# Image attention: the last 32 keys of four sub-steps gathered by GpSimd and turned by one transpose, and ScalarE evicts a transpose ahead of the next exponential

## The chip, the cores and the metric

The kernel runs on one core of a Trainium2 chip. The metric is the device time in microseconds (us) of one execution. TensorE (PE; its weight loads are shown apart as PEld), VectorE (DVE), ScalarE (ACT), GpSimd (POOL) and SyncE (SP) each run their own instructions in program order, and wait for each other by semaphores.

## The reference, cut to what matters

A chain of eight blocks (four cross-attentions, four feed-forward parts) updates x (4 batches of 512 tokens of 128 channels). The change touches the first block alone, an attention of 16 heads of 64 channels. Its queries come from x; its keys and values from the 154 context rows and the 512 rows of x together, so each query weighs 666 keys:

```python
kv_in = jnp.concatenate([x, l], axis=1)          # 154 context rows, 512 rows of x
k, v = jnp.split(kv_in @ Wkv, 2, axis=-1)        # 16 heads of 64
w = jnp.einsum('bhqd,bhkd->bhqk', q * scale, k * scale)
w = jax.nn.softmax(w, axis=-1)                   # over 666 keys
out = jnp.einsum('bhqk,bhkd->bhqd', w, v)
...
x = x + tanh(g_xattn[0]) * (out @ Wo)
```

## The kernel before, in words

This attention is called the image stage. Its work is cut into **sub-steps**, numbered i = 0 to 255: one sub-step is 128 queries of one head of one batch against all 666 keys. Four sub-steps (two heads h, two query tiles j) make a **unit** u, two units a **group** n (a pair of heads, `image_sub`). Keys are numbered 0 to 511 for x and 512 to 665 for the context, cut into KT0 = 6 tiles of 128; the sixth holds the last 26 keys. Values, scaled queries and probabilities are held in two bf16 parts, a high one and a low one (the remainder), and every product is the sum of three matmuls; "low" in a name is the remainder.

Every engine runs one loop over steps i (`image_steps`), and what it does in a step belongs to different sub-steps, so the pipeline is written out by hand. In step i:

- **PE** (`image_pe`): the scores of sub-step i into bank pair i % 2 (L683); in steps with i % 4 = 0 half of the weighing of unit i // 4 - 2 (tiles 0 to 2, L709, 18 matmuls), and in steps with i % 4 = 2 the other half (tiles 3 to 5, L709, 18 matmuls), then two transposes of the row of 1/sum (L615); then six transposes of the probabilities of sub-step i - 2 (`image_turn_pe`, L694: four into bank 4, two into bank 5); in even steps a quarter of the projections of the next group (L475, into bank 7, `side`).
- **DVE** (`image_ve`): in steps with i % 4 = 3 first the product with 1/sum (L740, `mixed`, which waits for ACT's `spread_kept`); then the row maximum of the scores of i (L744); in odd steps the remainders of the quarter that was projected (L798 to L813, `image_lows_ve`); in steps with i % 4 = 0 the reciprocal of the sums (L752, `inverted`); then the copy of bank 5 (L758, `kept_b`, 128x256), and for the first sub-step of a unit the remainder as well (L763, `low_c`).
- **ACT** (`image_ac`): the exponential of i (L837), which waits for DVE's maximum; in steps with i % 4 = 2 `spread_kept` (L846); the copy of bank 4 for sub-step i - 2 (L852, `kept_a`, 128x512); in even steps the quarter that was projected (L881 to L895).
- **POOL** (`image_po`): in steps with i % 4 = 0 first 1/sum spread over the heads' columns (L934, which waits for DVE's reciprocal) and the remainder of `mixed` (L942); then the remainders of the probabilities of sub-step i - 3 (L963: `low_a` 128x512, and `low_b` 128x256 in three of four sub-steps); then, in steps with i % 4 = 0 from 32 on, a piece of splitting the next block's weights (L979 to L983, 16 chunks in all).

For most steps nothing else is issued. A few hold **chores** (`image_chores`, `image_late`): the two normalizations of the next batch, its columns, the output projection of a batch that is done, and, near the end, the first routing steps of the next block. By their tables they touch 20 of the 64 units.

A step's name below is i % 4: **step 2** is the one with the second half of the weighing, and it turns a sub-step with i % 4 = 0. **Step 1** turns the fourth sub-step of a unit.

## Time and profile before

| | us |
|---|---|
| median of 3 runs | 1929.69 |
| lowest and highest | 1927.9 and 1934.78 |
| the profiled execution, its own time | 1934.83 |
| its span | 1933.0 |
| image stage, first to last exponential | 36.5 to 706.6 |
| PE busy in the span | 1515.4 (78%) |
| DVE, ACT, POOL busy in the span | 1205.2, 802.1, 757.9 |

In the views below an operation stands with its line, its engine, what it writes and reads, and its shape. A time in brackets behind it is the idle time of its engine just before it, with the work that ended that idle time. Starts are microseconds from the start of the span. A row of several instructions ("x6") spans from the first one's start to the last one's end, and the next row can start up to 0.1 us earlier than that, since an engine's operations overlap a little.

### The profile page before, as it was taken

To read this page: it belongs to the slowest core of one execution; us is meant where nothing else is said; L and a number is where in the kernel's file an instruction comes from. 1 tells how busy PE (TensorE), PEld (TensorE's weight loads), DVE (VectorE), ACT (ScalarE), POOL (GpSimd) and SP (SyncE) were. 2 spreads that over 40 slices of the span, in tenths; PEclk is the share of its full clock that TensorE was granted. 3 is DMA by queue.
4 is the path that set the end of the run, shared out by engine and by line. 5 is a ranking of instruction groups with operands and counts; after the bars stand their busy time and mean duration, and the time that the engine had idled before them with its cause. 6 is when DMAs were issued, how large, how long until landed. Compare 5 with 4: busy or idle time off the path is not lost.

```text
span 1933.0 us, 32091 instructions
## 1 busy us (share of the span) xinstructions
PE 1515.4 (78%) x11458; PEld 990.6 (51%) x11581; DVE 1205.2 (62%) x2958; ACT 802.1 (41%) x1806; POOL 757.9 (39%) x909
## 2 busy tenths in 40 slices
PE   4899989979998986574268789958976886478877
PEld 2677757766776665452155345523443333334544
DVE  5777667767766655547947657644465465676653
ACT  3677557747765644320035245533212452211111
POOL 3788668858755863510012342000002101143320
PEclk9999989999998997776558799989985697779887
DMA  6223211211211102400000000000000000000000
GB/s 243 76 87 106 76 52 42 55 35 41 53 38 42 51 20 84 150 20 1 0 1 1 11 4 2 1 1 1 1 1 1 1 1 1 1 1 6 1 6 12
DMA packets 35443, 63.94 MB, mean 33 GB/s; under 512 B 7527, under 2 KB 25026, under 8 KB 34131
## 3 DMA queue, kind: packets, MB, share of 16 engines
q1 hardware_dynamic: 33815, 59.77, 10.3%
q0 software_dynamic: 1472, 2.12, 0.3%
q8 instruction: 95, 1.56, 0.3%
q14 instruction: 61, 0.50, 0.1%
HBM read 30.59 MB, written 12.66 MB: 22 GB/s over the span
## 4 chain that ended last, share of the span: by engine, by line
PE 62%; DVE 24%; POOL 5%; issue 5%; ACT 3%; DMA 1%; SPq 0%; DVEq 0%; ACTq 0%; POOLq 0%
PE banks L475 14%; PE banks L694 8%; PE banks L709 6%; PE banks L683 6%; PE banks L1876 4%; DVE xn L421 3%; PE banks L1859 2%; PE banks L450 2%; POOL work L963 2%; PE banks L1785 1%; DVE norm_room L405 1%; PE banks L1826 1%; DVE work L744 1%; PE banks L2565 1%; PE banks L1516 1%
## 5 line engine op out<-in xcount | busy, mean ns | idle before, releaser
L963 POOL TENSOR_TENSOR work<-work 128x512 bf16<-128x512 f32 (+1 forms) x448 | 373.2, 863 | 47.6 <-ACT work L852 44.4
L837 ACT ACTIVATE work<-banks,work 128x666 f32<-128x666 f32 x256 | 209.2, 817 | 198.7 <-DVE work L744 163.3
L415 POOL TENSOR_TENSOR norm_room<-norm_room,minus_half 128x4 f32<-128x4 f32 x48 | 50.2, 1046 | 537.7 <-DVE norm_room L410 537.6
L744 DVE TENSOR_REDUCE work<-banks 128x1 f32<-128x666 f32 x256 | 216.1, 844 | 60.6 <-PE banks L683 60.1
L694 PE MATMUL banks<-const,work 128*128 128x128 f32 (+1 forms) x1536 | 218.5, 279 | 30.0 <-ACT work L852 25.8
L758 DVE COPY work<-banks 128x256 f32<-128x256 f32 x256 | 106.7, 417 | 123.7 <-PE banks L694 123.5
L694 PEld LDWEIGHTS banks<-const,work 128*128 128x128 f32 (+1 forms) x1536 | 156.5, 135 | 51.9 <-ACT work L837 29.3
L683 PE MATMUL banks<-work 128*128 128x154 bf16 (+1 forms) x932 | 172.2, 304 | 7.8 <-DMA work<-work 2.6
L475 PE MATMUL banks<-work,weights_b 128*128 128x512 bf16 (+1 forms) x830 | 157.2, 347 | 12.8 <-DVE work L2200 5.5
L709 PE MATMUL banks<-work 128*64 128x256 bf16 x2304 | 160.7, 284 | 7.5 <-POOL work L963 6.3
L852 ACT ACTIVATE work<-banks 128x512 f32<-128x512 f32 x256 | 151.3, 591 | 10.1 <-PE banks L694 9.8
L450 PE MATMUL banks<-const,xn 128*128 128x128 f32 x176 | 42.2, 385 | 135.8 <-DVE xn L421 83.8
L683 PEld LDWEIGHTS banks<-work 128*128 128x128 bf16 x1024 | 98.8, 99 | 86.0 <-issue 6.8
L456 ACT ACTIVATE xt<-banks 128x512 f32<-128x512 f32 x48 | 28.6, 597 | 267.8 <-PE banks L450 267.7
L1953 DVE TENSOR_REDUCE work<-banks 128x2 f32<-128x308 f32 x192 | 86.5, 472 | 83.2 <-PE banks L1831 45.3
L709 PEld LDWEIGHTS banks<-work 128*64 128x64 bf16 x2304 | 121.6, 111 | 28.3 <-POOL work L963 9.5
L475 PEld LDWEIGHTS banks<-work,weights_b 128*128 128x128 bf16 (+1 forms) x840 | 82.8, 100 | 83.1 <-issue 18.3
L2772 POOL TENSOR_TENSOR work<-work 128x512 bf16<-128x512 f32 x64 | 67.7, 1061 | 139.1 <-DVE work L2721 139.0
L1932 ACT ACTIVATE work<-banks 128x256 f32<-128x256 f32 (+1 forms) x256 | 87.4, 382 | 61.4 <-PE banks L1863 26.9
L450 PEld LDWEIGHTS banks<-const,xn 128*128 128x128 f32 x176 | 27.7, 193 | 148.5 <-DVE xn L421 77.6
L1859 PE MATMUL banks<-work 128*128 128x256 bf16 (+1 forms) x256 | 66.9, 293 | 14.4 <-ACT work L1924 11.6
L475 PE MATMUL banks<-weights_c 128*128 128x128 bf16 (+2 forms) x288 | 66.3, 261 | 0.0
(398 smaller groups left out, 3059.7 us busy)
## 6 DMA issues: line engine op xcount, KB each, us to landing
work<-work SPq DMA_DIRECT2D x128, 166.5 KB, 3.0
sorted<-in_pads SPq DMA_DIRECT2D x10, 838.5 KB
weights_b<-in_weights SPq DMA_DIRECT2D x1, 4120.0 KB, 23.4
work<-scratch SPq DMA_DIRECT2D x64, 64.0 KB, 2.0
weights_b<-in_weights SPq DMA_DIRECT2D x1, 2824.0 KB, 9.6
weights_a<-in_weights SPq DMA_DIRECT2D x1, 2056.0 KB, 8.1
weights_a<-in_weights SPq DMA_DIRECT2D x1, 2050.0 KB, 9.4
work<-work SPq DMA_DIRECT2D x32, 64.0 KB, 1.9
```

The costliest lines, as they stand in the source:

```text
L450: i = pe.transpose(ps[:, j * P:j * P + rows], src[0:rows, j, :], self.eye[0:rows, 0:rows])
L475: m = pe.matmul(out, left(a), right(b), start=start and n == 0, stop=stop and n == 2)
L683: m = pe.matmul(slot[:, a:z], lhs, k[:, h, part, a:z], start=part == 0, stop=part == 1)
L694: m = pe.transpose(ps[0:rows, c:c + P], prob[:, t * P:t * P + rows], self.eye)
L709: m = pe.matmul(self.out_bank[64 * h:64 * h + 64, 0:2 * P], self.v[n % 3][:, t, of_values, 64 * h:64 * h + 64], self.probs_parts[u % 2][:, ...
L744: ve.tensor_reduce(self.neg_max[i % 4], self.slot[i % 2][:, 0:KEYS0], AX_X, ALU.max, negate=True).then_inc(self.mark("max"))
L758: ve.tensor_copy(self.probs_t[u % 2][:, h, 4:KT0, j * P:(j + 1) * P], self.bank_b[:, 0:2 * P].rearrange("p (t n) -> p t n", t=2)).then_inc ...
L837: ac.activation(self.probs[i % 3], self.slot[i % 2][:, 0:KEYS0], ACT.Exp, bias=self.neg_max[i % 4], accum_out=self.sums[u % 4][:, 2 * j + ...
L852: ac.activation(self.probs_t[u % 2][:, h, 0:4, j * P:(j + 1) * P], self.bank_a.rearrange("p (t n) -> p t n", t=4), ACT.Copy).then_inc(self ...
L963: po.tensor_tensor(parts[:, :, :, 0], exact, parts[:, :, :, 1], ALU.subtract).then_inc(self.mark(event, i - 3))
L1859: m = pe.matmul(bank, left, a.q4[b % 2][:, g, cols], start=True, stop=s != 4)
L1932: ac.activation(out, self.bank_of(k, HALF)[0:rows_n, :], ACT.Exp).then_inc(self.mark("exp4", s, n))
```

## The change

Four things change, all of them in the image stage.

1. **The keys are cut in another way.** Tile 4 holds keys 512 to 633 (its other rows of values are zero), and the last 32 keys (634 to 665) are taken out. After the exponential of each sub-step, POOL copies its last 32 columns into 32 of the 128 columns of `rest` (L988 of the new kernel, `gathered`). When the fourth is there, one transpose turns all 128 (L700), in step 1, beside the fourth sub-step's own. A sub-step has five transposes of its own and no longer six.
2. **The weighing of these keys** is six matmuls of 128x128 over 128 columns for the unit (L722), in place of six of 64 columns of weights over 256 columns. The values lie in two extra tiles, zero outside of four blocks of 32x64 (`value_pieces`), so ACT and DVE each write five pieces in place of two in the third quarter of the projections. For each batch POOL lays the last 32 context columns out four times (`four_times`, two copies).
3. **Bank 5** holds one turned tile (128x128), copied by DVE for each sub-step, and in step 1 the gathered one, which DVE copies and takes the remainder of. POOL's `low_b` is 128x128, now for all four sub-steps. The exponential of i waits for `gathered` of i - 3, since the buffers of the probabilities take turns.
4. **ACT** issues `kept_a` of sub-step i - 2 ahead of the exponential of i, no longer behind it and behind `spread_kept`.

The diff, cut to its core:

```diff
@@ image_turn_pe
-        for bank, tiles, name in ((4, range(0, 4), "kept_a"), (5, range(4, KT0), "kept_b")):
-            ps = self.bank(pe, bank, *((name, i) if bank == 4 or (i % 4) else ("low_c", i // 4)))
...
+        ps = self.bank(pe, 4, "kept_a", i)
+        for t in range(4):
+            m = pe.transpose(ps[:, t * P:(t + 1) * P], prob[:, t * P:(t + 1) * P], self.eye)
+        m.then_inc(self.mark("turned_a"))
+        ps = self.bank(pe, 5, *(("kept_b", i) if i % 4 < 3 else ("low_c", i // 4)))
+        m = pe.transpose(ps[:, 0:P], prob[:, 4 * P:5 * P], self.eye)
+        if i % 4 == 3:
+            pe.wait_ge(*self.at("gathered", i))
+            m = pe.transpose(ps[:, P:2 * P], self.rest[i // 4 % 2], self.eye)
+        m.then_inc(self.mark("turned_b"))
@@ image_weigh_pe
-        if tiles[-1] == KT0 - 1:
+        if tiles[-1] == KT0 - 2:
+            rest = self.halves(self.rest_t[u % 2])
+            for of_values, of_probs in orders:
+                for j in (0, 1):
+                    m = pe.matmul(self.out_bank[:, j * P:(j + 1) * P], self.v[n % 3][:, KT0 - 1 + j, of_values, :], rest[:, :, of_probs],
...
@@ image_ve
-                ve.tensor_copy(self.probs_t[u % 2][:, h, 4:KT0, j * P:(j + 1) * P],
...
+                ve.tensor_copy(self.probs_t[u % 2][:, h, 4, j * P:(j + 1) * P], self.bank_b[:, 0:P]).then_inc(self.mark("kept_b", i - 2))
+                if (h, j) == (1, 1):
+                    whole = self.rest_t[u % 2]
+                    ve.wait_ge(*self.own("ve", ve.tensor_copy(whole, self.bank_b[:, P:2 * P])))
+                    ve.tensor_tensor(self.halves(whole)[:, :, 0], self.bank_b[:, P:2 * P], self.halves(whole)[:, :, 1],
                                      ALU.subtract).then_inc(self.mark("low_c", u))
@@ image_ac
         for i in self.image_steps():
+            if 2 <= i < SUBS + 2:
+                u, _, _, _, h, j = self.image_sub(i - 2)
...
+                ac.activation(self.probs_t[u % 2][:, h, 0:4, j * P:(j + 1) * P],
+                              self.bank_a.rearrange("p (t n) -> p t n", t=4), ACT.Copy).then_inc(self.mark("kept_a", i - 2))
             if i < SUBS:
                 u, _, _, _, h, j = self.image_sub(i)
                 if i >= 3:
                     ac.wait_ge(*self.at("turned_b", i - 2))
+                    ac.wait_ge(*self.at("gathered", i - 3))
@@ image_po
-                for tiles, event in (((0, 4), "low_a"), ((4, KT0), "low_b")):
+                for tiles, event in (((0, 4), "low_a"), ((4, KT0 - 1), "low_b")):
                     if event == "low_b":
-                        if (h, j) == (0, 0):
-                            continue
...
+            if 1 <= i < SUBS + 1:
+                u, s = (i - 1) // 4, (i - 1) % 4
+                if s == 0 and u >= 2:
+                    po.wait_ge(*self.at("turned_b", 4 * u - 4))
+                po.wait_ge(*self.at("exp", i))
+                po.tensor_copy(self.rest[u % 2][:, 32 * s:32 * (s + 1)], self.probs[(i - 1) % 3][:, KEYS0 - 32:]).then_inc(self.mark("gathered", i - 1))
@@ image_lows_ve (image_keep_ac likewise)
+            for tile, rows, cols, src in self.value_pieces():
+                ve.tensor_tensor(v[rows, tile, 1, cols], side[rows, src], v[rows, tile, 0, cols], ALU.subtract).then_inc(self.mark("v_low"))
+    def value_pieces(self):
+        out = [(KT0 - 2, slice(0, CTX - 32), slice(0, P), slice(2 * P, 3 * P))]
+        for h, j in ((0, 0), (0, 1), (1, 0), (1, 1)):
+            r, c = 32 * (2 * h + j), 64 * h
+            out.append((KT0 - 1 + j, slice(r, r + 32), slice(c, c + 64), slice(3 * P + c, 3 * P + c + 64)))
+        return out
```

ACT, end of step 1 to step 2 of one unit, before (L837 exponential, L852 `kept_a`, L846 `spread_kept`, L895 a projected quarter):

```order
199 L852 ACTIVATE work<-banks 128x4x128 [waits turned_a,weighed]
200 L837 ACTIVATE work<-banks,work 128x666 [waits max,turned_b]
201 L846 ACTIVATE work<-banks 128x256 [waits spread_turned]
202 L852 ACTIVATE work<-banks 128x4x128 [waits turned_a,weighed]
203 L895 ACTIVATE work<-banks 128x4x128 [waits projected]
```

The same place of the changed kernel (L861 exponential, L851 `kept_a`, L870 `spread_kept`, L912 the quarter):

```order
200 L861 ACTIVATE work<-banks,work 128x666 [waits max,low_b,turned_b]
201 L851 ACTIVATE work<-banks 128x4x128 [waits turned_a,weighed]
202 L861 ACTIVATE work<-banks,work 128x666 [waits max,low_b,turned_b]
203 L870 ACTIVATE work<-banks 128x256 [waits spread_turned]
204 L912 ACTIVATE work<-banks 128x4x128 [waits projected]
```

In step 2 `kept_a` stood third, behind the exponential and `spread_kept`; it stands first now, and both stand behind it.

POOL, step 0 of one unit and its weight piece, before (L934 spread of 1/sum, L942 remainder of `mixed`, L963 remainders of probabilities):

```order
108 L934 COPY work<-work 128x256 [waits inverted,spread_turned]
109 L942 TENSOR_TENSOR work<-work 128x256 [waits mixed]
110 L963 TENSOR_TENSOR work<-work 128x4x128 [waits kept_a]
111 L963 TENSOR_TENSOR work<-work 128x2x128 [waits kept_b]
112 L979 CAST split<-weights_b 128x512 [waits split]
```

The same place of the changed kernel (L953, L961, L982 are those three lines, L988 the gathering copy):

```order
159 L953 COPY work<-work 128x256 [waits inverted,spread_turned]
160 L961 TENSOR_TENSOR work<-work 128x256 [waits mixed]
161 L982 TENSOR_TENSOR work<-work 128x4x128 [waits kept_a]
162 L982 TENSOR_TENSOR work<-work 128x128 [waits kept_b]
163 L988 COPY work<-work 128x32 [waits exp]
164 L1013 CAST split<-weights_b 128x512 [waits split]
```

The copy that gathers a unit's fourth sub-step stands behind the four others of step 0.

PE, from the transposes of step 1 to the second half of the weighing in step 2, before:

```order
573 L694 MATMUL banks<-const,work 128x128 [waits kept_a,exp]
574 L694 MATMUL banks<-const,work 128x128 x3
575 L694 MATMUL banks<-const,work 128x128 [waits kept_b]
576 L694 MATMUL banks<-const,work 26x128
577 L683 MATMUL banks<-work 128x512 [waits exp,dma_head01]
578 L683 MATMUL banks<-work 128x512
579 L683 MATMUL banks<-work 128x154 x2
580 L709 MATMUL banks<-work 64x256 [waits low_c,low_b]
581 L709 MATMUL banks<-work 64x256 x17
582 L615 MATMUL banks<-const,work 128x128 [waits spread]
```

The same place of the changed kernel (`gathered` counts on the semaphore `low_b`):

```order
555 L694 MATMUL banks<-const,work 128x128 [waits kept_a,exp]
556 L694 MATMUL banks<-const,work 128x128 x3
557 L697 MATMUL banks<-const,work 128x128 [waits kept_b]
558 L700 MATMUL banks<-const,work 128x128 [waits low_b]
559 L686 MATMUL banks<-work 128x512 [waits exp,dma_head01]
560 L686 MATMUL banks<-work 128x512
561 L686 MATMUL banks<-work 128x154 x2
562 L716 MATMUL banks<-work 64x256 [waits low_c,low_b]
563 L716 MATMUL banks<-work 64x256 x11
564 L722 MATMUL banks<-work 128x128 x6
565 L616 MATMUL banks<-const,work 128x128 [waits spread]
```

The sixth transpose of step 1 waits for POOL's copy, and the scores of the next step stand behind it.

## Rows read from the trace of the kernel before

**Rows 1.** Windows: stretch, length, busy of PE, PEld, DVE, ACT, POOL; PEclk; DMA.
```profile
30.00:716.00 686.00, 621.61 (x6091) 471.98 (x6189) 472.83 (x1033) 447.12 (x1029) 500.89 (x649) 0.97 0.20 56
...
215.00:220.00 5.00, 4.19 (x44) 3.35 (x45) 2.33 (x5) 2.19 (x5) 1.94 (x3) 1.00 0.01 2
```

**Rows 2.** One line of code: L846 on ACT, one instruction a unit.
```profile
L846 ACT ACTIVATE work<-banks x64: 372/375/385, 66.2 to 715.7; 128x256 f32<-128x256 f32 x64
```

**Rows 3.** Timeline of ACT (start, length, line, shape, idle before): two L846.
```profile
75.97 0.38 ACT L846 ACTIVATE work<-banks 128x256 f32<-128x256 f32 x1
...
204.35 0.38 ACT L846 ACTIVATE work<-banks 128x256 f32<-128x256 f32 x1
```

**Rows 4.** Timeline of PE's weight loads, one unit from 302.60.
```profile
302.60 0.61 PEld L694 LDWEIGHTS banks<-const,work 128*128 128x128 f32 x6
...
307.23 0.59 PEld L694 LDWEIGHTS banks<-const,work 128*128 128x128 f32 x6 [0.35 <-issue]
...
309.09 0.60 PEld L694 LDWEIGHTS banks<-const,work 128*128 128x128 f32 x6
309.70 0.64 PEld L683 LDWEIGHTS banks<-work 128*128 128x128 bf16 x4
310.47 0.94 PEld L709 LDWEIGHTS banks<-work 128*64 128x64 bf16 x18
...
311.81 0.61 PEld L694 LDWEIGHTS banks<-const,work 128*128 128x128 f32 x6
```

**Rows 5.** Timeline of ACT in step 2 of that unit.
```profile
302.79 0.82 ACT L837 ACTIVATE work<-banks,work 128x666 f32<-128x666 f32 x1 [0.30 <-DVE work L744]
...
303.59 0.38 ACT L846 ACTIVATE work<-banks 128x256 f32<-128x256 f32 x1
303.86 0.60 ACT L852 ACTIVATE work<-banks 128x512 f32<-128x512 f32 x1
304.34 0.61 ACT L895 ACTIVATE work<-banks 128x512 bf16<-128x512 f32 x1
305.72 0.82 ACT L837 ACTIVATE work<-banks,work 128x666 f32<-128x666 f32 x1 [0.78 <-DVE work L744]
```

**Rows 6.** Timeline of DVE from step 2 to step 0 of that unit.
```profile
303.60 0.42 DVE L758 COPY work<-banks 128x256 f32<-128x256 f32 x1 [0.90 <-PE banks L694]
...
304.40 0.41 DVE L740 TENSOR_TENSOR work<-banks,work 128x256 f32<-128x256 f32 x1
304.78 0.85 DVE L744 TENSOR_REDUCE work<-banks 128x1 f32<-128x666 f32 x1
305.54 0.68 DVE L798 TENSOR_TENSOR work<-banks,work 128x512 bf16<-128x512 f32 x1
306.14 0.41 DVE L758 COPY work<-banks 128x256 f32<-128x256 f32 x1
306.47 0.84 DVE L744 TENSOR_REDUCE work<-banks 128x1 f32<-128x666 f32 x1
307.23 0.17 DVE L752 RECIPROCAL work<-work 128x4 f32<-128x4 f32 x1
```

**Rows 7.** Timeline of POOL in step 0 of that unit.
```profile
307.53 0.40 POOL L934 COPY work<-work 128x256 f32<-128x256 f32 x1 [1.44 <-DVE work L752]
307.89 0.62 POOL L942 TENSOR_TENSOR work<-work 128x256 bf16<-128x256 f32 x1
308.46 1.62 POOL L963 TENSOR_TENSOR work<-work 128x512 bf16<-128x512 f32 x2
310.01 0.61 POOL L979 CAST split<-weights_b 128x512 bf16<-128x512 f32 x1
```

**Rows 8.** Groups by shape, to 850 us: count, busy us, mean ns, idle before.
```profile
L963 POOL TENSOR_TENSOR work<-work 128x512 bf16<-128x512 f32 x256 | 267.8, 1046 | 47.6 <-ACT work L852 44.4
L963 POOL TENSOR_TENSOR work<-work 128x256 bf16<-128x256 f32 x192 | 119.0, 620 | 0.0
...
L921 POOL COPY context<-work 128x616 f32<-128x616 f32 x2 | 1.3, 701 | 0.0
```

More of the change, by code:

```diff
@@ L522, in image_memory @@
         self.k = [self.place(2, 2, KEYS0, dt=BF16) for _ in range(2)]
-        self.v = [self.place(KT0, 2, P, dt=BF16) for _ in range(3)]
+        self.v = [self.place(KT0 + 1, 2, P, dt=BF16) for _ in range(3)]
         self.probs = [self.place(KEYS0) for _ in range(3)]
@@ L526, in image_memory @@
         self.q_part = self.scratch[:, 2:4, :].rearrange("p t n -> p (t n)").bitcast(BF16)
-        self.probs_t = [self.place(2, KT0, 2 * P) for _ in range(2)]
+        self.probs_t = [self.place(2, KT0 - 1, 2 * P) for _ in range(2)]
+        self.rest, self.rest_t = ([self.place(P) for _ in range(2)] for _ in range(2))
         self.sums = [self.place(4) for _ in range(4)]
+        self.ctx_last = self.place(2, P, dt=BF16)
         self.inverse = [self.place(4) for _ in range(2)]
@@ L595, in image_pe @@
         pe.wait_ge(*self.at("dma_const", 16))
-        pe.wait_ge(*self.at("clean", 1))
         self.turn(pe, ("in", 0), self.xn[:, 0:QT, :], 0, ("in", 0, 1))
@@ L654, in image_project_pe @@
         elif part == 2:
-            self.bank(pe, 7, "v_low", 3 * n + 2)
+            self.bank(pe, 7, "v_low", 6 * n + 5)
             if n == 0:
@@ L662, in image_project_pe @@
             self.products(pe, side[:, 2 * P:3 * P], lambda s: c[:, s, c0:c0 + P], lambda s: values[s], True, True)
-            m = self.products(pe, side[:, 3 * P:4 * P], lambda s: c[:, s, c0 + P:c0 + 2 * P], lambda s: values[s], True, True)
+            if n % PAIRS == 0:
+                pe.wait_ge(*self.at("four_times", b))
+            m = self.products(pe, side[:, 3 * P:4 * P], lambda s: self.ctx_last[:, s, :], lambda s: values[s], True, True)
         else:
-            self.bank(pe, 7, "v_low", 3 * n + 3)
+            self.bank(pe, 7, "v_low", 6 * n + 6)
             for t in range(QT):
@@ L688, in image_turn_pe @@
         pe.wait_ge(*self.at("exp", i + 1))
-        for bank, tiles, name in ((4, range(0, 4), "kept_a"), (5, range(4, KT0), "kept_b")):
-            ps = self.bank(pe, bank, *((name, i) if bank == 4 or (i % 4) else ("low_c", i // 4)))
-            for t in tiles:
-                rows = min(P, KEYS0 - t * P)
-                c = (t - tiles[0]) * P
-                m = pe.transpose(ps[0:rows, c:c + P], prob[:, t * P:t * P + rows], self.eye)
-            m.then_inc(self.mark("turned_a" if bank == 4 else "turned_b"))
+        ps = self.bank(pe, 4, "kept_a", i)
[8 more added lines that the diff above has]
+        m.then_inc(self.mark("turned_b"))
     def image_weigh_pe(self, pe, u, tiles):
@@ L891, in image_keep_ac @@
                 v = self.v[n % 3]
-                ac.activation(v[:, 4, 0, :], side[:, 2 * P:3 * P], ACT.Copy).then_inc(self.mark("v_kept"))
-                ac.activation(v[0:CTX_REST, 5, 0, :], side[0:CTX_REST, 3 * P:4 * P], ACT.Copy).then_inc(self.mark("v_kept"))
+                for tile, rows, cols, src in self.value_pieces():
+                    ac.activation(v[rows, tile, 0, cols], side[rows, src], ACT.Copy).then_inc(self.mark("v_kept"))
         else:
@@ L967, in image_po, with four_times_po @@
             pass
+    def four_times_po(self, po, b):
+        if b:
+            po.wait_ge(*self.at("projected", 4 * (PAIRS * b - 1) + 3))
+        for s in (0, 1):
+            i = po.tensor_copy(self.ctx_last[:, s, :].rearrange("p (r k) -> p r k", r=4),
+                               self.ctxn_parts[:, s, (b + 1) * CTX - 32:(b + 1) * CTX].unsqueeze(1).to_broadcast([P, 4, 32]))
+        i.then_inc(self.mark("four_times", b))
     def image_x_low_po(self, po, b):
```

48 lines of the change are left out of this document (20 added, 28 removed).

## The prediction

> **What bounds the kernel now.** I read the windows first. Over the image stage PE is busy 621.61 of 686.00 us and POOL 500.89, DVE 472.83, ACT 447.12, at a granted clock of 0.97 [rows 1]. So PE is the busiest, but a change that lengthens a chain of waits between the engines can still take its place. The pace comes from `spread_kept`, which ACT issues once a unit: 64 of them from 66.2 to 715.7 us, so 10.31 us from one to the next on average [rows 2]. Where no chores fall, 14 units take 128.38 us, 9.17 us each [rows 3]. By the chores' tables 20 of the 64 units hold chores; 44 are clean.
>
> In a clean unit PE's weight loads follow each other nearly without a gap: from one step 2's first transpose to the next it is 302.60 to 311.81, 9.21 us, and the only gaps that a row names are 0.35 us ahead of the transposes of step 0 and one of 0.2 us inside the 1.34 us from the second half of the weighing to the transposes of step 2 (1.34 less 0.94 of loads and 0.20 for two transposes) [rows 4]. PE sets the pace there, and everything else has slack.
>
> **The change part by part.**
>
> *Transposes.* Six take 0.60 us, 309.09 to 309.70, or 0.10 each [rows 4]. Three of four sub-steps lose one; the fourth keeps six. That is 0.30 us a unit off the bounding engine.
>
> *Weighing.* 18 matmuls over 256 columns take 0.94 us of loads, 0.052 us each, and two of them run side by side in halves of the array [rows 4]. Six of the old form go, and six full-width ones over 128 columns come: the same number of columns through the array when pairs overlap. I take nothing, with 0.1 us a unit either way. The row shows a switch from half-width to full-width at about 0.2 us, and the change moves it from behind 18 matmuls to behind 12. The Trainium skill, TensorEngine Tiling (Array Packing), section Key Properties, says that a change of tiling mode drains the engine; by it alone a second drain would come if the six counted as another mode than the transposes behind them, and the sum would be 0.2 us a unit higher. The rows show none between bf16 and f32 work of full width: the loads of L683 begin 0.01 us after those of L694 end [rows 4].
>
> *ACT's order, seen from PE.* The gap of 0.35 us in step 0 [rows 4] is partly the wait for bank 4, which `kept_a` frees late because it stands behind an exponential that waits for DVE. With `kept_a` first it shrinks to the drain, 0.2: 0.14 us a unit. So **the gain is 0.44 us a unit**, if nothing else becomes late.
>
> *What becomes late: ACT.* In step 2 the first operation is now `kept_a`, which needs four transposes of that step. PE does them behind the weighing. In the trace DVE's copy of bank 5 starts 1.00 us after the first of six [rows 4, 6], so `kept_a` can start 0.80 after it (two transposes fewer), at 303.40 on the clock of before. The exponential had started at 302.79 [rows 5]; it now starts at 303.40 + 0.48 = 303.88, over a microsecond later. Behind it stands `spread_kept`, for it DVE's product (L740) waits at the head of step 3, and behind that both maxima, the reciprocal, and POOL's whole step 0. This is the wait that the change adds, and its queue.
>
> *What becomes late: POOL.* The sixth transpose of step 1 waits for a copy that POOL makes last in step 0. POOL begins that step only after DVE's reciprocal, even before the change [rows 7].
>
> *The loop.* These join into one chain which closes on itself in one unit. Each term is a distance between starts unless stated:
> - PE's first transpose in step 2 to `kept_a`: 0.80 (above); to the exponential: 0.48 (303.86 to 304.34 [rows 5]); to `spread_kept`: 0.80 (302.79 to 303.59 [rows 5]); its length 0.38 and the handover 0.09 (DVE's maximum ends at 305.63, ACT starts at 305.72 [rows 5, 6]): 2.55.
> - DVE [rows 6]: product 0.38, maximum 0.76, remainder of the quarter 0.60, copy of bank 5 0.33 less 0.13, maximum 0.76: 2.70. The 0.13 is my estimate for half the columns, the slope between 0.41 us for 256 columns and 0.85 for 666 being 1.07 ns a column. Reciprocal to POOL 0.30 [rows 6, 7]: 3.00.
> - POOL [rows 7, 8]: spread 0.36, remainder of `mixed` 0.57, the pair of remainders 1.55. The pair's second is 128x128 now: 1046 ns for 512 columns and 620 for 256 give 1.66 ns a column, so 0.21 less, 1.34. The gathering copy: 398 ns for 256 columns (the 0.40 of the row) and 701 for 616 give 0.21 us for 32. Sum 2.48.
> - Handover to PE 0.10, then the sixth transpose 0.10, scores 0.77, weighing, drain and 1/sum 1.34 [rows 4]: 2.31, and PE is at the first transpose of step 2 again.
>
> 2.55 + 3.00 + 2.48 + 2.31 = **10.34 us a unit**, against 9.17 now and 8.73 that PE would need. PE stands about 1.6 us in each unit at the sixth transpose; the 0.44 us that it saved is in that wait. +1.17 us x 44 clean units = 51 us. In the other 20, DVE's chores already keep PE waiting, and a part of the chain is hidden under them; bounds are 0 and 1.17 each, and I take the middle, 12 us. The five small pieces (three more instructions on ACT and on DVE in one quarter a group) lie where both have slack in this loop. Start and end of the stage: under 2 us. Sum +63: the profiled execution would go from 1934.83 to 1998, and the median, 5.1 lower, from 1929.69 to **1993**.
>
> Bounds. The copy can be 0.15 to 0.40 (its slope without a floor is under 0.05, and the whole 256-column one is 0.40), `low_b` between 0.41 and its old 0.62, DVE's copy between 0.20 and 0.33, the six matmuls 0.1 either way: T from 10.2 to 10.9. With 0 to the full rise in the 20 units: 1929.69 + 44 x 1.0 = 1974 up to 1929.69 + 64 x 1.7 = 2038; both ends at once are unlikely, and I keep 1974 to 2022 for this case.
>
> **The rivals.**
>
> *The gathering copy alone is late.* If the later exponential does not reach DVE's product in time to matter, the loop starts at the scores of step 3: maximum to POOL is 0.76 + 0.60 + 0.20 + 0.76 + 0.30 = 2.62, POOL and handover 2.58, PE to step 2's transposes 2.21, from them to the maximum's start 302.60 to 304.78 less one transpose, 2.08: 9.49 us [rows 4, 6, 7]. +0.32 x 44 and some in the rest: **1947**. Against it: nothing in the code lets L740 pass ahead of `spread_kept`, nor that ahead of the exponential. It holds if ACT's `kept_a` starts far sooner than 0.80 us after the first transpose.
>
> *PE stays the bound: faster.* 8.73 us a unit, -0.44 x 44 and half of it in the others: 19 + 4, **1906**. This needs the copy ready when PE has done five transposes of step 1, at 309.60 on the old clock. On that clock POOL starts step 0 at 307.53 and needs 2.48, so 310.0 at best; it decides from 0.4 us less on POOL. For it speaks only that POOL idles 1.44 us ahead of the step [rows 7], but it idles waiting for DVE.
>
> *No change.* The waits take just what the transposes give, as when POOL's step 0 is 0.3 us shorter than I have and the product is not late: **1930**.
>
> *The clock falls.* A PE that stands 15% of the time might be granted less. A window with 4.19 of 5.00 us busy still has 1.00 [rows 1], and the loop has 8.73 of 10.34, the same share. If it fell to half, PE would be the bound again far above 2022.
>
> **How the numbers follow.** The main case gets 0.66, the copy alone 0.13, PE the bound 0.11, no change 0.07, the clock or something worse than my bounds 0.03. The range that leaves out no more than 0.2 runs from 1942 to 2022: the main case and the copy alone. About 0.5% (10 us) is what a measurement of this kernel can tell from no change. Faster by more: 0.11; within: 0.07; slower: 0.82.
>
> **What the profile after would show.** `spread_kept` once every 10.3 us in clean stretches; PE's weight loads idle 1.3 to 1.8 us in front of the sixth transpose of step 1, released by POOL's copy; DVE idle ahead of the product for ACT's `spread_kept`, and no longer ahead of the maximum of step 3; ACT idle ahead of `kept_a` for PE's transposes; POOL's 128x32 copy at 0.2 us. If PE's wait is about 0.5 us and DVE starts step 3's maximum as the scores end, the second case holds. If no wait is there, POOL's step 0 began sooner than the reciprocal of before allowed, and I am wrong on DVE's order. The likeliest error of size is what the 20 units with chores do.

## The result, and the profile after

| | before | after |
|---|---|---|
| median, us | 1928.80 (1927.62 to 1934.78, 4 runs) | 1986.99 (1984.81 to 1991.53, 4 runs) |
| profiled execution, us | 1934.83 | 1984.81 |
| its span, us | 1933.0 | 1983.0 |

The ratio of after to before is 1.0303, with a 95% interval of 1.0288 to 1.0319. The change makes the kernel 3% slower. The forecast was 1993 us, in a range of 1942 to 2022.

From the page of the kernel after, parts 1, 4 and 5 (line, engine, operation, out<-in, count | busy us, mean ns of one | idle before and its releaser):

```profile
PE 1508.4 (76%) x11389; PEld 971.1 (49%) x11389; DVE 1194.2 (60%) x3117; ACT 816.3 (41%) x1902; POOL 780.4 (39%) x1237
...
PE 46%; DVE 26%; POOL 10%; issue 9%; ACT 6%; DMA 1%; ACTq 0%; SPq 0%; DVEq 0%; POOLq 0%
...
L851 ACT ACTIVATE work<-banks 128x512 f32<-128x512 f32 x256 | 154.3, 603 | 215.4 <-PE banks L694 214.4
```

PE still has most work, yet its share of the chain that ended last is 46% now, against 62% on the page of before. ACT idles 214 us in all in front of `kept_a` (L851), waiting for PE's transposes. The same two views as in [rows 1] and [rows 2], of after (windows: stretch, length, busy of PE, PEld, DVE, ACT, POOL, then PEclk; and one line of code):

```profile
30.00:716.00 686.00, 570.47 (x5573) 422.85 (x5574) 435.23 (x1127) 429.31 (x1050) 487.17 (x905) 0.97 0.20 55
...
L870 ACT ACTIVATE work<-banks x64: 374/384/386, 69.3 to 766.7; 128x256 f32<-128x256 f32 x64
```

All five engines are less busy in the same 686 us, PE by 51, and the granted clock is the 0.97 of before. Over the whole span PE and DVE have 7 and 11 us less work than before, ACT and POOL 14 and 22 us more, on engines that are busy less than half of the time. That doesn't make 50 us: the engines wait for each other. `spread_kept` starts its 64 units at 69.3 and ends them at 766.7, 697.4 us against 649.5 before [rows 2]. The difference is 48 us; 3 more are lost ahead of the first one. That is the 50 us by which the profiled executions differ.

Now one clean unit, link by link. PE's weight loads (start, length, line, shape, idle before with its releaser), from one step 2 to the next:

```profile
324.81 0.47 PEld L694 LDWEIGHTS banks<-const,work 128*128 128x128 f32 x4
...
329.05 0.42 PEld L694 LDWEIGHTS banks<-const,work 128*128 128x128 f32 x4 [0.20 <-issue]
...
331.20 0.14 PEld L697 LDWEIGHTS banks<-const,work 128*128 128x128 f32 x1
332.80 0.14 PEld L700 LDWEIGHTS banks<-const,work 128*128 128x128 f32 x1 [1.46 <-POOL work L988]
332.88 0.63 PEld L686 LDWEIGHTS banks<-work 128*128 128x128 bf16 x4
333.63 0.59 PEld L716 LDWEIGHTS banks<-work 128*64 128x64 bf16 x12
334.43 0.34 PEld L722 LDWEIGHTS banks<-work 128*128 128x128 bf16 x6 [0.21 <-issue]
334.73 0.20 PEld L616 LDWEIGHTS banks<-const,work 128*128 128x128 f32 x2
334.90 0.47 PEld L694 LDWEIGHTS banks<-const,work 128*128 128x128 f32 x4
```

ACT, DVE and POOL in the same unit:

```profile
325.61 0.60 ACT L851 ACTIVATE work<-banks 128x512 f32<-128x512 f32 x1 [1.79 <-PE banks L694]
326.11 0.81 ACT L861 ACTIVATE work<-banks,work 128x666 f32<-128x666 f32 x1
...
326.90 0.38 ACT L870 ACTIVATE work<-banks 128x256 f32<-128x256 f32 x1
```

```profile
327.31 0.42 DVE L750 TENSOR_TENSOR work<-banks,work 128x256 f32<-128x256 f32 x1 [1.29 <-ACT work L870]
327.65 0.84 DVE L754 TENSOR_REDUCE work<-banks 128x1 f32<-128x666 f32 x1
328.41 0.68 DVE L815 TENSOR_TENSOR work<-banks,work 128x512 bf16<-128x512 f32 x1
329.01 0.28 DVE L768 COPY work<-banks 128x128 f32<-128x128 f32 x1
329.21 0.84 DVE L754 TENSOR_REDUCE work<-banks 128x1 f32<-128x666 f32 x1
329.97 0.17 DVE L762 RECIPROCAL work<-work 128x4 f32<-128x4 f32 x1
```

```profile
330.26 0.40 POOL L953 COPY work<-work 128x256 f32<-128x256 f32 x1 [2.10 <-DVE work L762]
330.63 0.62 POOL L961 TENSOR_TENSOR work<-work 128x256 bf16<-128x256 f32 x1
331.20 1.40 POOL L982 TENSOR_TENSOR work<-work 128x512 bf16<-128x512 f32 x2
332.54 0.21 POOL L988 COPY work<-work 128x32 f32<-128x32 f32 x1
```

Read them as one ring: PE turns (324.81), ACT copies bank 4 (325.61), takes the exponential (326.11), writes `spread_kept` (326.90); DVE multiplies (327.31), finds a maximum, works off a quarter, copies bank 5, finds a second maximum, inverts (329.97); POOL does its step 0 (330.26) and the gathering copy last (332.54); PE, which has stood 1.46 us, makes the sixth transpose (332.80), the scores, the weighing, and turns again (334.90). Each idle time in the ring is released by the link ahead of it. It takes 10.09 us, and in the long stretches without chores nearly every unit has 10.09 or 10.10. An early unit, the one that ends with the `spread_kept` of 112.95 us, has one more operation on POOL ahead of the copy (L956, 1.04 us), and takes 11.09: 1.00 more, as a link of the ring would.

### The profile page after: what moved, and what is told of

The parts are those of the page before. It is cut to its first block, busy times and chain, and to the rows that moved or that the text cites. A ratio compares the mean times of both kernels' runs of the same rounds, so it can differ in the third digit from the quotient of the medians.

```text
span 1983.0 us, 32535 instructions
## 1 busy us (share of the span) xinstructions
PE 1508.4 (76%) x11389; PEld 971.1 (49%) x11389; DVE 1194.2 (60%) x3117; ACT 816.3 (41%) x1902; POOL 780.4 (39%) x1237
## 3 DMA queue, kind: packets, MB, share of 16 engines
q1 hardware_dynamic: 33815, 59.77, 10.1%
## 4 chain that ended last, share of the span: by engine, by line
PE 46%; DVE 26%; POOL 10%; issue 9%; ACT 6%; DMA 1%; ACTq 0%; SPq 0%; DVEq 0%; POOLq 0%
PE banks L475 11%; PE banks L1910 3%; POOL work L982 3%; PE banks L716 3%; ACT work L861 3%; DVE xn L421 3%; DVE work L754 2%; PE banks L686 2%; PE banks L1893 2%; PE banks L450 2%; POOL work L961 2%; PE banks L1819 1%; PE banks L694 1%; DVE norm_room L405 1%; PE banks L1860 1%
## 5 line engine op out<-in xcount | busy, mean ns | idle before, releaser
L982 POOL TENSOR_TENSOR work<-work 128x512 bf16<-128x512 f32 (+1 forms) x512 | 360.2, 728 | 32.3 <-ACT work L851 29.8
L851 ACT ACTIVATE work<-banks 128x512 f32<-128x512 f32 x256 | 154.3, 603 | 215.4 <-PE banks L694 214.4
L861 ACT ACTIVATE work<-banks,work 128x666 f32<-128x666 f32 x256 | 208.6, 815 | 37.5 <-DVE work L754 37.1
L686 PE MATMUL banks<-work 128*128 128x512 bf16 (+1 forms) x1024 | 191.1, 310 | 4.3 <-DMA work<-work 3.6
L694 PE MATMUL banks<-const,work 128*128 128x128 f32 x1024 | 160.7, 280 | 2.7 <-ACT work L851 2.7
L716 PE MATMUL banks<-work 128*64 128x256 bf16 x1920 | 138.8, 286 | 6.1 <-POOL work L982 4.2
L686 PEld LDWEIGHTS banks<-work 128*128 128x128 bf16 x1024 | 99.2, 100 | 85.9 <-issue 6.5
L768 DVE COPY work<-banks 128x128 f32<-128x128 f32 x256 | 72.1, 282 | 99.1 <-PE banks L697 61.6
L694 PEld LDWEIGHTS banks<-const,work 128*128 128x128 f32 x1024 | 114.1, 143 | 17.2 <-issue 15.9
L2806 POOL TENSOR_TENSOR work<-work 128x512 bf16<-128x512 f32 x64 | 67.7, 1061 | 138.8 <-DVE work L2755 138.6
L716 PEld LDWEIGHTS banks<-work 128*64 128x64 bf16 x1920 | 100.2, 110 | 25.1 <-POOL work L982 7.2
L700 PE MATMUL banks<-const,work 128*128 128x128 f32 x64 | 21.2, 332 | 89.0 <-POOL work L988 89.0
L953 POOL COPY work<-work 128x256 f32<-128x256 f32 x64 | 25.7, 402 | 136.8 <-DVE work L762 136.8
```

The source lines that it names most:

```text
L686: m = pe.matmul(slot[:, a:z], lhs, k[:, h, part, a:z], start=part == 0, stop=part == 1)
L694: m = pe.transpose(ps[:, t * P:(t + 1) * P], prob[:, t * P:(t + 1) * P], self.eye)
L716: pe.matmul(self.out_bank[64 * h:64 * h + 64, 0:2 * P], self.v[n % 3][:, t, of_values, 64 * h:64 * h + 64], self.probs_parts[u % 2][:, h, ...
L768: ve.tensor_copy(self.probs_t[u % 2][:, h, 4, j * P:(j + 1) * P], self.bank_b[:, 0:P]).then_inc(self.mark("kept_b", i - 2))
L851: ac.activation(self.probs_t[u % 2][:, h, 0:4, j * P:(j + 1) * P], self.bank_a.rearrange("p (t n) -> p t n", t=4), ACT.Copy).then_inc(self ...
L861: ac.activation(self.probs[i % 3], self.slot[i % 2][:, 0:KEYS0], ACT.Exp, bias=self.neg_max[i % 4], accum_out=self.sums[u % 4][:, 2 * j + ...
```

## The experiments

Each kernel differs from the one named by the edit shown. Medians differ by up to 9 us from chip to chip (1928.58 to 1937.41 for before), so times are compared through the ratio to runs of before on the same chip. The length of a unit is read from ACT's timeline, from one `spread_kept` to the next.

### The two halves of the change apart

**e1: after, with ACT's order as before.**

```
 for i in self.image_steps():
-    kept_a of step i-2
     exponential of step i
     spread_kept
+    kept_a of step i-2
```

> The changed kernel with kept_a back behind the exponential and spread_kept, all else kept. Theory (one loop through ACT's order and through POOL's gathering copy, 10.10 us a clean unit): without ACT's part the loop starts at the scores of step 3, 2.61 on DVE + 2.28 on POOL + 0.26 handover + 2.10 to the transposes of step 2 + 2.01 to the next maximum = 9.26 us a clean unit, total 1935 to 1945 us, PE still stands 0.4 to 0.6 us at the sixth transpose. Rival A (the copy alone makes the loss): stays near 1987. Rival B (ACT's order alone makes it): back to 1929 or, with the transposes saved, 1910.

Measured: ratio 1.0136 (1.0099 to 1.0173), or 1955 us on the 1928.80 of before, above the range that I had expected. Units of 9.25 and 9.97 us alternate. The short one has the length expected, but e4 below has it too, without the copy at the end of POOL's step: the agreement with 9.26 does not show that the copy sets it. The long one I had not foreseen. It comes in units with the five pieces of values. PE's loads, ACT and DVE in a long unit of e1, on the way to its long wait:

```profile
216.60 0.42 PEld L694 LDWEIGHTS banks<-const,work 128*128 128x128 f32 x4 [0.95 <-ACT work L854]
```

```profile
211.94 1.16 DVE L830 TENSOR_TENSOR work<-banks,work 122x128 bf16<-122x128 f32 x5
213.13 0.29 DVE L768 COPY work<-banks 128x128 f32<-128x128 f32 x1
...
213.86 0.84 DVE L754 TENSOR_REDUCE work<-banks 128x1 f32<-128x666 f32 x1
```

```profile
214.82 0.81 ACT L854 ACTIVATE work<-banks,work 128x666 f32<-128x666 f32 x1 [1.51 <-DVE work L754]
...
215.89 0.60 ACT L869 ACTIVATE work<-banks 128x512 f32<-128x512 f32 x1
```

DVE has the five pieces, three operations on the turned keys and then the maximum of step 2. ACT's exponential (L854) stands 1.51 us for that maximum, and `kept_a` (L869) behind it keeps bank 4 from PE in step 3. PE's row names the exponential, but that had ended at 215.63; PE starts at 216.60, 0.11 us after the end of `kept_a`. So the gathered tile makes a second queue, on DVE, beside the copy on POOL.

**e2: before, with `kept_a` first.** The same move, the other way, on the kernel before.

> The kernel of before with only ACT's order changed (kept_a ahead of the exponential). Theory: DVE's product and POOL's step 0 come over a microsecond later, but PE waits for neither without the gathered transpose, so PE stays the bound, 9.03 to 9.17 us a clean unit, 1922 to 1930 us. Rival B (ACT's order alone makes the loss): about 1987, 10.1 us a unit.

Measured: ratio 0.9986 (0.9962 to 1.0010), clean units mostly of 8.87 to 9.25. The order that makes ACT's exponential a microsecond later costs nothing while nobody makes a ring of it. The 0.14 us at step 0 that the prediction gave it is there too, in PE's loads of e2:

```profile
477.90 0.59 PEld L694 LDWEIGHTS banks<-const,work 128*128 128x128 f32 x6 [0.21 <-issue]
```

The idle time is 0.21 us where [rows 4] has 0.35. With the gathering copy in place the same order costs 1.7% (1.0136 in e1 to 1.0303 in after). So ACT's order costs nothing alone and the gathering alone costs 1.4%; more than half of the 3% is there only with both together.

### The gathering copy

**e3: after, the copy at the head of POOL's step.**

```
 for i in self.image_steps():
+    wait for the exponential of step i-1; copy its last 32 keys
     spread; remainder of mixed
     pair of remainders of step i-3
-    wait for the exponential of step i-1; copy its last 32 keys
```

> The changed kernel with POOL's gathering copy moved to the head of its step, ahead of the spread of 1/sum and of the remainders. Theory: the copy is then ready when the exponential is, PE no longer stands at the sixth transpose, the 1.5 us of wait a unit goes and 8.6 to 8.8 us a clean unit are left (PE and POOL both near their limit): 1905 to 1918 us. Rival A' (PE stands there for ACT's or DVE's lateness, not for POOL's place in the order): above 1960.

Measured: ratio 1.0020 (0.9993 to 1.0048). The 3% are gone, and none of PE's loads of the sixth transpose waits any more, so the ring through the copy's place on POOL was the cause; the gain of the transposes was still not to be had. Clean units mostly alternate between 8.64, which is near the 8.73 forecast for PE alone, and 9.39, or 10.08 in place of 9.39 while POOL splits the second layer's weights.

In the long unit PE's fifth transpose waits for DVE. PE's loads of e3, then DVE and ACT ahead of it:

```profile
497.95 0.14 PEld L697 LDWEIGHTS banks<-const,work 128*128 128x128 f32 x1 [0.87 <-DVE work L772]
```

```profile
495.64 0.32 DVE L827 TENSOR_TENSOR work<-banks,work 128x154 bf16<-128x154 f32 x1 [0.57 <-ACT work L910]
495.88 1.16 DVE L830 TENSOR_TENSOR work<-banks,work 122x128 bf16<-122x128 f32 x5
497.07 0.29 DVE L768 COPY work<-banks 128x128 f32<-128x128 f32 x1
...
497.59 0.30 DVE L772 TENSOR_TENSOR work<-banks,work 128x128 bf16<-128x128 f32 x1
```

```profile
494.53 1.08 ACT L910 ACTIVATE work<-banks 122x128 bf16<-122x128 f32 x5
```

The five pieces take ACT 1.08 us and DVE 1.16, and DVE can't begin before ACT is through with them. Behind them stand the three operations that free bank 5 for PE.

**e10: after, the copy ahead of the pair only**, so that spread and remainder of `mixed` stay ahead of it.

> The changed kernel with POOL's copy ahead of the pair of remainders but still behind the spread of 1/sum and the remainder of mixed. By the loop's own sum this takes 1.34 us out of 10.10: 8.76 us for a short unit, where the loop still just binds (8.64 with the copy first), the long ones as with the copy first, 9.4 to 10.1; total 1930 to 1942 us. If the loop did not run through the pair, 10.10 would stay.

Measured: ratio 1.0066 (1.0045 to 1.0086); units 8.72 or 8.73 and 9.38, or 10.13 with weights. The short unit's sum was 8.76. PE still stands at the sixth transpose, about 0.1 us in a short unit and 0.53 in this one of 9.56:

```profile
306.31 0.14 PEld L700 LDWEIGHTS banks<-const,work 128*128 128x128 f32 x1 [0.53 <-POOL work L978]
```

**e5: after, the copy made twice**, the second behind a wait for the first.

> The changed kernel with POOL's gathering copy made twice in a row, the second after the first has ended (0.21 to 0.3 us more a sub-step on POOL). Theory (the copy closes the loop that sets the pace): a clean unit goes from 10.10 to 10.3 to 10.4 us, all units alike, and the total rises by 10 to 17 us. Rival A' (PE waits there for something else): 10.10 stays, since POOL idles 1.2 to 2.1 us a unit.

Measured: 2008.76 us in a single run, against 1937.03 for before on that chip: a ratio of 1.037, with no interval, some 13 us above the ratio of after and within the 10 to 17 expected. The clean units take 10.37, 0.27 more than after. POOL's timeline in e5, first copy and second:

```profile
306.47 0.21 POOL L988 COPY work<-work 128x32 f32<-128x32 f32 x1
306.74 0.21 POOL L989 COPY work<-work 128x32 f32<-128x32 f32 x1
```

They start 0.27 us apart, and the unit is longer by exactly that. What stands on POOL ahead of PE's sixth transpose is paid in full. PE's own work leaves 1.4 us a unit free, and that hides none of it.

### What makes every second unit long

**e4: e3 with ACT's order of before.** The edit is that of e1.

> The copy at the head of POOL's step, and kept_a behind the exponential as before the change. Theory: as the kernel with the copy first, but the wait for bank 4 in step 0 is back (0.14 us a unit, 6 to 9 us in all): 1911 to 1925 us. If ACT's order matters only inside the loop through the copy, it must come out within 10 us of that kernel.

Measured: ratio 1.0093 (1.0065 to 1.0120), units 9.25 and 9.97 as in e1. I had taken ACT's order for nearly free here as well, and missed. With the copy out of the way, the exponential of step 2 waits for DVE, `kept_a` stands behind the exponential, and PE waits for bank 4:

```profile
527.55 0.42 PEld L694 LDWEIGHTS banks<-const,work 128*128 128x128 f32 x4 [1.21 <-ACT work L854]
```

That is a second ring, and it sets the pace of e1 too. In the short unit its links are the same in both kernels: the exponential of step 2 to `kept_a` 1.07 us, to PE's transposes of step 3 0.71, to the scores of step 1 3.44, to their maximum 0.98, to the maximum of step 2 2.09, to the next exponential of step 2 0.96, together 9.25. In e4 no load of the sixth transpose waits; in e1 some wait 0.3 to 0.5 us for the copy, and it costs a clean unit nothing. With the copy first, ACT's new order is worth 0.7% (e4 to e3); with the copy last it costs 1.7%.

**e7 and e8: DVE's work on the turned keys behind step 2's maximum instead of ahead of it**, e7 on e4 and e8 on e3.

```
 # DVE
-step 1: copy and remainder of the gathered tile
 step 2: maximum
+step 2: copy and remainder of the gathered tile
```

> Copy first on POOL, ACT in its old order, and DVE's copy and remainder of the gathered tile moved from step 1 behind the maximum of step 2. Theory E (in ACT's old order these two operations, some 0.5 us, sit ahead of step 2's maximum, and through the exponential and kept_a hold PE's transposes of step 3; 9.25 and 9.97 us a pair of units): the pair falls by up to 0.5 us each, to 8.75 to 8.9 and 9.3 to 9.5, total 1925 to 1940 us. Rival: 9.25 and 9.97 stay, the later exponential comes from the pieces alone or from PE.

> The same with the changed kernel's order on ACT. Theory: with kept_a first, step 2's maximum has slack (the exponential waits behind kept_a anyway), so the short units keep 8.64; the long ones, where PE's fifth transpose of step 2 waits for the remainder, change by under 0.3 us. Total within 10 us of the kernel with the copy first, 1925 to 1942 us. If the remainder's place in step 1 is what makes the long units, they fall by 0.5 us and the total by 15.

Measured: e7 1.0080 (1.0056 to 1.0105), units 9.10 and 9.80, 0.15 better than e4 each and far less than expected. PE waits anew, for the remainder that was moved:

```profile
483.49 0.14 PEld L697 LDWEIGHTS banks<-const,work 128*128 128x128 f32 x1 [0.93 <-DVE work L807]
```

e8 1.0106 (1.0086 to 1.0126), units 8.97 and 9.92: worse than e3. PE's loads in e8:

```profile
312.20 0.14 PEld L697 LDWEIGHTS banks<-const,work 128*128 128x128 f32 x1 [1.70 <-DVE work L807]
```

L807 is the remainder that was moved. It frees bank 5 for PE's fifth transpose of step 2, which now waits 1.70 us; I had looked at the maximum alone. With five pieces ahead of them, the copy and the remainder can stand neither ahead of the maximum nor behind it without someone waiting.

**e6: e3 with two pieces of values in place of five.** This kernel leaves the spreading of the last 32 keys' values over their places undone, as its expectation says.

> The kernel with the copy first, and of the five pieces of the context values only two are written (the first tile, and all 128 rows of the second in one), on ACT and on DVE: the third value tile stays zero and the second holds what does not belong there, so the output is not the reference's. Theory C (with the copy out of the way, the five small pieces of the third quarter set every second unit, 9.39 to 10.08 us against 8.64): all clean units come near 8.64, where POOL's weight pieces allow it, and the total falls by 15 to 30 us against the kernel with the copy first. Rival D (the long units are long because of POOL's weight pieces or of the moved remainder alone): they stay above 9.3, total within 5 us.

Measured: ratio 0.9928 (0.9903 to 0.9952), units 8.52 and 8.65 where no weights are split. The long units of 9.39 are gone: the pieces made them. With weights, units of 9.2 stay, in which PE waits 0.8 us for POOL. Eight clean units of 9.1 to 10.1, with weights and without, are long for another reason: PE's loads for the scores (L686) stand 0.5 to 1.5 us for a DMA into `work`.

**e9: e3 with three pieces.** Two of the five copies write only half the columns of a row block, since each head has its own. Here PE makes the two heads' products from context rows with zeros in the other head's places, so that one copy takes 64 rows and all 128 columns.

```
-four pieces 32 rows x 64 columns, one a head and query tile
+two pieces 64 rows x 128 columns, one a query tile
-gathered rows: head, then query tile
+gathered rows: query tile, then head
```

> The kernel with the copy first, and the context values written in three pieces in place of five: GpSimd lays the last 32 context columns out once for each head with zeros for the other, PE multiplies each with its head's 64 columns, the gathered rows are ordered by query tile, so that each extra value tile is one piece of 64 rows. Nothing is left out. Theory C (pieces set every second unit): two pieces fewer on DVE and ACT are worth 0.3 to 0.45 us in each long unit, so these fall from 9.39 to 9.0 in the stretches without weight pieces, 8.64 stays in the short ones; total 8 to 14 us below the kernel with the copy first, so 0.3 to 0.7% below the kernel before. Rival: long units stay at 9.39, total as before.

Measured: ratio 0.9973 (0.9956 to 0.9990). Without weights the clean units take 8.63 to 8.66, but for one of 9.96. I had expected 9.0 of the long ones: the two pieces fewer took all of their 0.75 us. DVE begins its pieces only behind ACT's, so both savings count: ACT's went from 1.08 us to 0.72, DVE's from 1.16 to 0.80. While POOL splits weights, about one unit in three takes 9.1 to 9.3, three take 9.9 to 10.0, the others 8.6 to 8.9. In those three, and in the one of 9.96, PE's loads for the scores wait 1.31 to 1.44 us for a DMA; in the units of 9.1 to 9.3 PE waits for POOL. POOL's timeline in e9, and PE's wait at the first half of the weighing:

```profile
155.07 0.61 POOL L1018 CAST split<-weights_b 128x512 bf16<-128x512 f32 x1
155.76 1.17 POOL L1019 TENSOR_TENSOR split<-weights_b,split 128x512 bf16<-128x512 f32 x1
156.99 0.21 POOL L952 COPY work<-work 128x32 f32<-128x32 f32 x1
...
158.66 1.40 POOL L988 TENSOR_TENSOR work<-work 128x512 bf16<-128x512 f32 x2
```

```profile
159.75 0.94 PEld L718 LDWEIGHTS banks<-work 128*64 128x64 bf16 x18 [0.71 <-POOL work L988]
```

The weights that POOL splits at the end of step 0 hold it for 1.92 us, 155.07 to 156.99. The remainders for which the weighing (L718) waits are the pair of 158.66, two steps further on.

**e11: e9 with the pieces of the weights at the end of step 2. e12: before with the same move alone.**

```
-if i >= 32 and i % 4 == 0:
+if i >= 32 and i % 4 == 2:
     next(pieces, None)
```

> e9 with one thing changed: the pieces of the second layer's weights that POOL splits (CAST and subtraction, or the COPY that joins them) stand at the end of step 2 instead of the end of step 0. In e9 the clean units without such a piece take 8.65 us, those with one 9.3 to 10.0: some 12 units, 0.65 to 1.35 us each. Theory (the piece stands ahead of the copy at the head of step 1 and so holds the remainders for the weighing, which is why those units are long): in step 2 it stands behind the last remainder that the weighing needs, all clean units take 8.65, and the ratio to the kernel before falls by some 10 us, from 0.9973 to about 0.992. Rival (the long units come from PE's and DVE's work in the same units, and the weights are only in step with it by chance): the same units stay long, ratio 0.997.

> The kernel before with the same move alone of the pieces of the weights, from the end of step 0 to the end of step 2. In before the clean units take 9.17 us with and without a piece, since PE sets the pace there. So: no change, 1929 within 5 us, ratio 0.998 to 1.002. If it gains as much as e11 does over e9, that gain has nothing to do with the gathered keys.

Measured: e11 0.9914 (0.9882 to 0.9947), a median of 1920.11 against 1935.12 on that chip; e12 0.9988 (0.9968 to 1.0008). In the long stretches without chores all units of e11 but three take 8.63 to 9.06, nearly all of them 8.64 to 8.67. POOL and PE in e11 while weights are split:

```profile
338.03 1.40 POOL L988 TENSOR_TENSOR work<-work 128x512 bf16<-128x512 f32 x2
339.37 0.61 POOL L1018 CAST split<-weights_b 128x512 bf16<-128x512 f32 x1
340.06 1.16 POOL L1019 TENSOR_TENSOR split<-weights_b,split 128x512 bf16<-128x512 f32 x1
```

```profile
340.16 0.95 PEld L718 LDWEIGHTS banks<-work 128*64 128x64 bf16 x18
```

The last remainder is ahead of the weights now, and PE's weighing begins without a wait. In all three units of 9.9 or 10.0 that are left, PE waits for a DMA into `work`: 1.44 us in the row below, 1.32 at 349.44 and 1.44 at 493.42. In the last of them POOL splits no weights at all.

```profile
132.09 0.55 PEld L688 LDWEIGHTS banks<-work 128*128 128x128 bf16 x4 [1.44 <-DMA work<-work]
```

So one transpose in place of four does pay, 0.9% instead of costing 3%, once the copy, the pieces of values and the weights stand where they hold nobody. By e12 before gains at most 0.3% from the move of the weights, and its interval allows for no gain at all; the rest is the gathered keys' own.

## Why the prediction was right, and where its sizes were off

**PE bounded the kernel before, and the gain on PE.** Right. Where nothing else is late, as in the short units of e3 and most units of e11, a unit takes 8.64 to 8.66. The prediction had 8.73 for a PE that alone sets the pace. Before has 9.08 and 9.21 in turn, so the edit is worth 0.50 us a unit, not 0.44. The gap ahead of step 0's transposes fell from 0.35 [rows 4] to 0.20, as said. The rest is the weighing: from its start to the transposes of step 2 it takes 1.27 us (333.63 to 334.90) where it took 1.34 [rows 4]. I had put nothing, with 0.1 either way.

**The drain.** The rows of after show one, 0.21 us ahead of L722, and none ahead of L616 or of step 2's L694. The second drain that the Trainium skill's rule (TensorEngine Tiling (Array Packing), section Key Properties) would have brought if the six counted as another mode is not there; the sum without it holds.

**The chain.** Right link by link. The terms of the sum and what they measured, from the rows above:

| part | forecast | measured |
|---|---|---|
| PE's turn to `kept_a` | 0.80 | 0.80 |
| to the exponential, to `spread_kept` | 0.48, 0.80 | 0.50, 0.79 |
| to DVE's product | 0.47 | 0.41 |
| product, maximum, remainder, copy, maximum | 2.70 | 2.66 |
| reciprocal to POOL | 0.30 | 0.29 |
| POOL: spread, `mixed`, pair | 2.27 | 2.28 |
| copy and handover to PE | 0.31 | 0.26 |
| PE: transpose, scores, weighing | 2.21 | 2.10 |
| unit | 10.34 | 10.09 |

No term is wrong by more than 0.11, but the larger errors point the same way. A handover was taken as the length of an operation and a pause; in the trace the consumer starts 0.41 us after a producer of 0.38, and PE 0.26 after the start of POOL's copy of 0.21. Where the next start is all that matters, distances between starts have to be read, and I had them for most links and not for these two. Those two and PE's last link, of which 0.07 is the weighing, make 0.22 of the 0.25 us a unit, 11 us in 44 units. The length of DVE's copy of half the columns (0.28 us, as the slope gave) and 0.21 for POOL's 32 columns were right.

**The clock.** Right for the stage: 0.97 in the same window with PE 51 us less busy. In one short stretch the rival was there, though. From 85 to 90 us after was granted 0.74 where before had 1.00, so a part of it at the lower level of 1.2 GHz; just ahead of it PE had stood 2.46 us at the sixth transpose. The unit around it took 12.39 us.

**The 20 units with chores.** Forecast +12 us, measured +7: 649.5 less 44 units of 9.17 leaves 246 us before, and 697.4 less 44 of 10.10 leaves 253 after. That chores on DVE already kept PE waiting, and so hid a part of the ring, is likely but was taken apart by no run. The 7 also holds two early units without chores, 12.39 and 11.09, which POOL's extra operation and the clock made long by 2.3 and 1.0 beyond 10.10, and the last four of the stage, which grew by 0.7 in all where four clean ones would have grown by 3.7; the two about cancel.

**Start of the stage.** Forecast under 2 us, measured 3: the first `spread_kept` is at 69.3 for 66.2 [rows 2]. Among the experiments it lies at 69.4 to 69.7 in e2, e3, e8 and e11, and at 67.6 to 68.4 in e5, e6, e9 and e10, which have the same order on ACT; without it, in e1, e4, e7 and e12, at 67.5 to 68.3. In e12, whose code up to there is that of before, it is 67.7 where before has 66.2: half of the 3 us lies between two profiles of the same code. From 50 to 70 us the granted clock was 0.91 in before and 0.83 in e12 and in after. That leaves 1.6 us at most for the change, and no cause was shown for them. I had not walked through the filling of the pipe.

Clean units, chores and start add up to 41 + 7 + 3 = 51 us for the profiled execution, which went up by 50.0. The forecast had 63 for it. The medians moved by 58, since the profiled one of before is above its median and that of after below. That 1993 came within 6 us of 1987 is partly luck: the forecast was 13 us too high for the profiled execution, and the spread between runs gave 8 of them back.

**The pieces of values.** This step was true only for the kernel as it stood: "lie where both have slack in this loop". After shows no clean unit that they made long. In e3 the ring is gone, and the same pieces make every second unit 0.75 us longer. I had not asked what the slack would be in the case that I called PE the bound; that case, with 8.73 in all units and 1906 us, could not have come from moving the copy alone, and my expectation of e3, at 1905 to 1918, fell for the same reason.

**The rivals.** *The copy alone is late*, 1947 us by 9.49 a unit: e1 has exactly this, the copy last on POOL without the late exponential. It gave 9.25 and 9.97, 9.61 on average, and a ratio of 1.0136, or 1955 us on the 1928.80 of before. Neither is the rival's mechanism: e4, without the copy at the end, has the same 9.25 and 9.97, so in e1 the second ring, through DVE and ACT's old order, sets the pace, and the rival did not have that ring. That the short unit agrees with the 9.26 expected of e1 is luck, and no run shows the rival's own ring setting a pace. In after the rival fell since `kept_a` started 0.80 us after the first transpose, the very point named for it. *PE stays the bound*: the copy was ready 1.5 us too late; in e3 the bound is reached in every second unit. *No change* has nothing for it, *the clock* only the stretch named above.

**The signs.** All that were named are there: 10.1 for 10.3 between two `spread_kept`; PE idle 1.46 to 1.60 us at the sixth transpose, for POOL's copy; DVE idle ahead of the product and not ahead of step 3's maximum; ACT idle ahead of `kept_a`; the copy at 0.21. The view of the copy's line, L988, of after, with who waited for it (us, times):

```profile
L988 POOL COPY work<-work x256: 201/213/230, 38.3 to 760.9; 128x32 f32<-128x32 f32 x128
...
  PEld banks L700: 102.6, 58
```

PE's loads waited in 58 of the 64 units.

What stays open: why the DMA ahead of the three long units of e11 comes late; what the start of the stage hangs on; and how much of the 0.6% from e9 to e11 is the weights' own, since the two ran on different chips.

## What to carry to other kernels

When a change takes work off the engine that bounds the loop and hands a small part of it to another, follow that part back to what starts it and forward until it meets itself. If it closes, add up distances between starts, and compare the sum with the bounding engine's own pace: the ring wins by its length, however little each link is busy. Here a copy of 0.2 us had to go first in its engine's step, not last. A change of order that is free alone (e2) has to be priced again with the other half of the change in place. And a unit that comes out at the length of a ring's sum (e1) shows that ring only if taking a link out changes the length (e4).

## What the runs showed of the hardware that I had not expected

Small pieces have a price of their own, which falls little with what they hold. ACT's timelines of e6 (two pieces), e11 (three) and e3 (five, which stands above):

```profile
311.80 0.46 ACT L907 ACTIVATE work<-banks 122x128 bf16<-122x128 f32 x2
```

```profile
343.53 0.72 ACT L909 ACTIVATE work<-banks 122x128 bf16<-122x128 f32 x3
```

That is 0.23, 0.24 and 0.22 us from one to the next, though four of the five hold only 32x64. Singly, ACT's pieces of e3 last 0.21 us for 32x64 and 0.29 for 122x128, and DVE's 0.22 and 0.28. A whole quarter of 128x512 takes ACT 0.61 us [rows 5]. And PE's pause between half-width and full-width weights is 0.21 us behind 12 matmuls and 0.20 to 0.21 behind 18.
